# A three-sublayer block (routed attention, gated recurrence, routed attention): fp16 transposes moved from the matrix engine to the DMA queue, with a new order of the work

## The reference

```
x = x + 0.5 * ffn(layernorm(x), W_gate, W_qkv)
x = x + attn(layernorm(x), gamma, beta, W_in, b_in, W_out, b_out, W_skip, b_skip)
x = x + 0.5 * ffn(layernorm(x), W_gate, W_qkv)

ffn:   gating = softmax(x @ W_gate.T)              # 16 heads
       q, k, v = split(x @ W_qkv.T)
       k, v of the top-1 head of each row are kept (v times its gate)
       att = softmax(causal(q_h @ k_shared.T / 4)) # 16 heads of width 16
       y = att @ v_shared
attn:  u = layernorm(x) * gamma + beta
       delta, b, c = split(u @ W_in + b_in);  alpha = sigmoid(delta)
       h_t = (1 - alpha_t) h_(t-1) + alpha_t b_t;  y_t = h_t tanh(c_t)
       out = y @ W_out + b_out + x @ W_skip + b_skip
```

## Time and profile before

| | us |
|---|---|
| median of 3 runs (lowest, highest) | 844.35 (844.28, 846.64) |
| the profiled execution, its own time | 846.07 |
| its span, first to last instruction | 844.3 |
| PE matmul busy | 813.1 (96%) |
| DVE busy | 732.2 (87%) |
| ACT busy | 712.4 (84%) |
| POOL busy | 307.5 (36%) |
| mean granted TensorE clock | 0.985 of full speed |
| DMA queue of SP, share of 16 engines | 6.0% |

### The profile page before, as it was taken

One profiled execution on the slowest core, in us unless ns is written; L12 is line 12 of the kernel. 1 busy time (PEld: TensorE's weight loads), 2 busy tenths in 40 slices (PEclk: granted clock), 3 DMA queues, 4 the chain that ended last, 5 costly groups with the idle time before them and its releaser, 6 DMA issues.

```text
span 844.3 us, 18872 instructions
## 1 busy us (share of the span) xinstructions
PE 813.1 (96%) x6416; PEld 282.2 (33%) x6416; DVE 732.2 (87%) x2315; ACT 712.4 (84%) x1130; POOL 307.5 (36%) x600
## 2 busy tenths in 40 slices
PE   9999999999999999999999999999999999999997
PEld 6533333333232232324233433342223333222221
DVE  5889899899999999999738996999999899999910
ACT  1148797869999789897989898899998899999996
POOL 3235524623224433236545365631124434011010
PEclk9889799999999999999999999999999999999999
DMA  6120001111000000100020002000000100000000
GB/s 200 51 64 2 2 2 30 36 33 33 2 2 2 1 2 2 58 7 2 2 64 1 3 3 63 2 2 26 2 2 15 52 26 28 1 2 2 1 1 26
DMA packets 20254, 18.00 MB, mean 21 GB/s; under 512 B 4144, under 2 KB 20160, under 8 KB 20160
## 3 DMA queue, kind: packets, MB, share of 16 engines
q1 hardware_dynamic: 19072, 15.74, 6.0%
q10 hardware_dynamic: 1088, 1.07, 0.4%
HBM read 10.24 MB, written 6.29 MB: 20 GB/s over the span
## 4 chain that ended last, share of the span: by engine, by line
PE 57%; DVE 16%; issue 9%; ACT 9%; POOL 7%; DMA 1%; SPq 0%; POOLq 0%; ACTq 0%; DVEq 0%
PE ps L1715 19%; PE ps L1680 12%; PE ps L1703 10%; ACT probs L1191 6%; DVE mxp L1406 6%; DVE ps L1409 5%; PE ps L1598 3%; ACT relu L1175 2%; PE ps L1613 2%; POOL u L876 2%; PE ps L1646 1%; DMA q_t<-m_row 1%; POOL u_x L942 1%; DVE mxp L1409 1%; PE ps L1603 1%
## 5 line engine op out<-in xcount | busy, mean ns | idle before, releaser
L1191 ACT ACTIVATE probs<-ps 128x1024 f32<-128x1024 f32 (+4 forms) x763 | 546.6, 800 | 54.5 <-PE ps L1703 50.3
L1715 PE MATMUL ps<-probs,v_l 128*32 128x512 f32 (+3 forms) x2560 | 296.3, 544 | 1.4 <-ACT probs L1191 0.7
L1406 DVE TENSOR_REDUCE mxp<-ps 128x1 f32<-128x512 f32 x384 | 240.8, 683 | 8.9 <-PE ps L1680 5.5
L1409 DVE CUSTOM_DVE_ANT_0 ps<-ps,mask 128x384 f32<-128x384 f32 (+3 forms) x512 | 233.8, 524 | 15.5 <-PE ps L1680 14.2
L1680 PE MATMUL ps<-k_tl,q_t 48*128 48x512 f16 (+3 forms) x1152 | 227.3, 336 | 5.7 <-DVE mxp L1409 2.5
L1703 PE MATMUL ps<-q_t,k_tl 50*128 50x512 f16 (+3 forms) x1280 | 220.5, 353 | 9.6 <-DMA q_t<-m_row 2.2
L911 POOL TENSOR_SCALAR_AFFINE_SELECT probs<-probs 128x256 f32<-128x256 f32 (+1 forms) x192 | 92.4, 488 | 226.9 <-ACT probs L1191 225.0
L1409 DVE CUSTOM_DVE_ANT_0 ps<-ps,relu 128x256 f32<-128x256 f32 (+1 forms) x256 | 136.3, 587 | 5.8 <-PE ps L1680 5.0
L1680 PEld LDWEIGHTS ps<-k_tl,q_t 48*128 48x128 f16 x1152 | 70.4, 94 | 152.0 <-DVE mxp L1409 40.2
L1703 PEld LDWEIGHTS ps<-q_t,k_tl 50*128 50x128 f16 x1280 | 62.1, 94 | 176.8 <-ACT probs L1191 92.5
L1175 ACT ACTIVATE relu<-ps 128x512 f32<-128x512 f32 x192 | 108.1, 620 | 5.0 <-PE ps L1680 4.5
(11 more groups left out here) (183 smaller groups left out, 638.0 us busy)
## 6 DMA issues: line engine op xcount, KB each, us to landing
q_t<-q_scratch SPq DMA_DIRECT2D x96, 64.0 KB, 2.3
q_scratch<-q_part SPq DMA_DIRECT2D x16, 256.0 KB, 2.2
out_dram<-x_sb SPq DMA_DIRECT2D x4, 512.0 KB, 3.5
x_sb<-in_L_attn_x_dram SPq DMA_DIRECT2D x3, 512.0 KB, 5.1
q_t<-m_row SPq DMA_DIRECT2D x64, 4.0 KB
wqkv_n<-in_L_ffn_W_qkv_dram ACTq DMA_DIRECT2D x1, 768.0 KB, 5.3
w_in_sb<-in_L_attn_W_in_dram SPq DMA_DIRECT2D x1, 384.0 KB, 5.6
x_sb<-in_L_attn_x_dram ACTq DMA_DIRECT2D x1, 256.0 KB, 3.4
```

The source lines that it names most:

```text
L1191: last = a_.activation(out[:, done:done + banks], scores, ACT.Exp, scale=SCALE / LIFT ** 2)
L1406: last = v_.tensor_reduce(to, scores, axis=AX, op=ALU.max)
L1409: last = v_.tensor_tensor_reduce(scores, scores, added, 1.0, LOWEST, ALU.add, ALU.max, accum_out=to)
L1715: last = mm(out_bank[VW * hh:VW * hh + VW, P * i:QW], v_l[:, l, kt, :], probs[:, s % NB, hh, P * i:QW], start=j == 0, stop=j == key_tiles( ...
```

## The change

All fp16 transposes leave PE. A new entry `flip` transposes both halves of a normed chunk at once, by one transposing DMA issued from SP (`dma_start_transpose`, [128, 2048] fp16); `keys` and `dkeys` become transposing DMAs on SP as well (512 or 256 columns), and `row` too, for which `mx2` is widened to 128 columns; the two small DMAs that followed it are now an entry of their own, `mrow`. The copies by ACT go with them. The fp32 transposes of (0,0) and (0,1) stay on PE. POOL no longer waits for PE's transposes before it overwrites `u` or `mx2`, but for the halves or for the transposing DMA. Halves are laid out as `[2, DC, TC, 128]`, so that what the DMA reads is contiguous. The planner's durations are set anew (one line of them is shown), it has SP as an engine, and `PICKS` is a new string (2408 entries for 2389).

```
+    flipped = [("turn", l, c, 0), ("turn", l, c, 1)] if (l, c) in SINGLE \
+        else [("halve", l, c, dc) for dc in range(DC)] + [("flip", l, c)]
+    return [("stats", l, c), ("norm", l, c)] + flipped + [("gate", l, c), ("pick", l, c),
...
-    return [("stats", 2, c), ("norm", 2, c), ("halve", 2, c, 0), ("halve", 2, c, 1), ("turn", 2, c, 0), ("turn", 2, c, 1), ("bsum", c, 0), ("bsum", c, 1),
+    return [("stats", 2, c), ("norm", 2, c), ("halve", 2, c, 0), ("halve", 2, c, 1), ("flip", 2, c), ("bsum", c, 0), ("bsum", c, 1),
...
-    "gate": (1850, [("DVE", 450), ("ACT", 250)]), "pick": (0, [("DVE", 1400)]),
+    "gate": (1810, [("DVE", 395), ("ACT", 250)]), "pick": (0, [("DVE", 1550)]),
...
-TURN_MODE, ROW_TRIP, QUERY_TRIP = 97, 2300, 6000
+TURN_MODE = 97
+LANDING = {"flip": 2300, "keys": 2000, "dkeys": 2000, "row": 2000, "mrow": 2300, "qout": 2300, "qin": 2300}
...
-    "55222222222225522252555422225522205255520050240222052200552122202212201115220312420225511002112200235422222022",
+    "5zd22222225222222552252224245550252244500522002102212255522224505055042111202202102225320225104141100535022122",
...
-        rows.append(("row", u))
+        rows += [("row", u), ("mrow", u)]
...
-        mx2 = sb("mx2", [P, 2 * GH * TC], f16)
-        m_row = sb("m_row", [2 * GH * TC, 2, P], f16)
+        mx2 = sb("mx2", [P, P], f16)
+        m_row = sb("m_row", [P, 2, P], f16)
...
+                elif e[0] == "flip":
+                    _, l, c = e
+                    sp.wait_ge(s_half, NO["halve", l, c, DC - 1] + 1)
+                    if FLIP_BEFORE[e]:
+                        past = FLIP_BEFORE[e][2]
+                        sp.wait_ge(s_fill, filled(("skip", past, 1) if l == 2 else ("kv", FLIP_BEFORE[e][1], past, TC - 1)))
+                    to = u2t_x if l == 2 else ut_x
+                    sp.dma_start_transpose(to[:, :, :, :].rearrange("p a d (t x) -> p (a d t) x", x=P),
+                                           u_x[:, :, :, :, :].rearrange("p a d t x -> p (a d t x)")).then_inc(s_flip, 16)
+                elif e[0] == "keys":
+                    _, l, c = e
+                    sp.wait_ge(s_krow, prep_no(l, c) + 1)
+                    sp.dma_start_transpose(k_tl[:, l, c, :].rearrange("p (t x) -> p t x", x=P),
+                                           k_rows[:, :, :].rearrange("p t x -> p (t x)")).then_inc(s_kt, 16)
+                elif e[0] == "dkeys":
+                    _, l, c = e
+                    sp.wait_ge(s_drow, NO[e] + 1)
+                    to = (kd_tl if c else kh_tl)[:, l, :]
+                    sp.dma_start_transpose(to.rearrange("p (t x) -> p t x", x=P),
+                                           k_rows[:, 0:to.shape[1] // P, :].rearrange("p t x -> p (t x)")).then_inc(s_kt, 16)
                 elif e[0] == "row":
+                    v = e[1]
+                    sp.wait_ge(s_mx, v + 1)
+                    if v >= 2:
+                        sp.wait_ge(s_md[v % 2], 32 * (v // 2))
+                    sp.dma_start_transpose(m_row[:, v % 2:v % 2 + 1, :], mx2[:, :]).then_inc(s_row, 16)
+                elif e[0] == "mrow":
                     l, c, g = UNITS[e[1]]
-                    sp.wait_ge(s_ra, FREED[e])
+                    sp.wait_ge(s_row, 16 * (e[1] + 1))
...
-                if k:
-
-                    pool.wait_ge(s_fill, filled(TURNS[k - 1]))
+                if k and fine(*NORMS[k - 1][1:]):
+                    pool.wait_ge(s_half, NO[("halve",) + NORMS[k - 1][1:] + (DC - 1,)] + 1)
...
-                    pool.wait_ge(s_fill, filled(("row", v - 1)))
+                    pool.wait_ge(s_row, 16 * v)
...
+                if NO["flip", l, c]:
+
+                    pool.wait_ge(s_flip, 16 * NO["flip", l, c])
+                whole, first = u[:, :, dc * P:(dc + 1) * P], u_x[:, 0, dc, :, :]
                 own(g_.tensor_copy(first, whole))
-                g_.tensor_tensor(u_x[:, 1, :, dc * P:(dc + 1) * P], whole, first, op=ALU.subtract).then_inc(s_half, 1)
+                g_.tensor_tensor(u_x[:, 1, dc, :, :], whole, first, op=ALU.subtract).then_inc(s_half, 1)
...
-                elif e[0] == "turn" and fine(e[1], e[2]):
-                    dst = u2t_x if e[1] == 2 else ut_x
-                    a_.activation(dst[:, e[3], :, :].rearrange("p a t -> p (a t)"), bank[:, :].bitcast(f16), ACT.Copy)\
-                        .then_inc(s_ra, 1)
...
-                elif e[0] == "keys":
-                    _, l, c = e
-                    a_.activation(k_tl[:, l, c, :], bank[:, 0:QW // 2].bitcast(f16), ACT.Copy).then_inc(s_ra, 1)
-                elif e[0] == "dkeys":
...
-                elif e[0] == "row":
-                    v = e[1]
-                    if v >= 2:
-                        act.wait_ge(s_md[v % 2], 32 * (v // 2))
-                    a_.activation(m_row[:, v % 2, :], as_rows(bank), ACT.Copy).then_inc(s_ra, 1)
...
-                        act.wait_ge(s_fill, filled(TURNED[e]))
+                        act.wait_ge(s_kt, 16 * KEYS_FLIPPED[e])
...
                 if fine(l, c):
-                    parts = bank.bitcast(f16)
-                    for a in range(2):
-                        for t in range(TC):
-                            last = tr(parts[:, a * QW + t * P:a * QW + (t + 1) * P], u_x[:, a, t, dc * P:(dc + 1) * P],
-                                      ident_h[:, :])
-                    last.then_inc(s_fill, 1)
-                    return
...
+                    pe.wait_ge(s_flip, 16 * (NO["flip", l, c] + 1))
+                    pe.wait_ge(s_wx, 3)
...
-                if e[0] == "row":
-                    pe.wait_ge(s_mx, v + 1)
-                    tr(as_rows(bank), mx2[:, :], ident_h[:, :]).then_inc(s_fill, 1)
-                    return
                 if e[2] == 0:
                     pe.wait_ge(s_qt[prep_no(l, c)][g // 2], 16 * 2 * len(Q_PART))
-                    pe.wait_ge(s_ra, FREED["keys", l, c])
+                    pe.wait_ge(s_kt, 16 * KEYS_FLIPPED["keys", l, c])
                     if c:
-                        pe.wait_ge(s_ra, FREED["dkeys", l, min(c, 2) - 1])
+                        pe.wait_ge(s_kt, 16 * KEYS_FLIPPED["dkeys", l, min(c, 2) - 1])
```

200 lines of the change are left out of this document (92 added, 108 removed).

## The result

The changed kernel is slower: 855.3 us median (852.8 to 857.9, 4 runs) against 845.5 (844.3 to 846.8, 4 runs), a ratio of 1.0122 with a 95% interval of 1.0095 to 1.0148. That is 1.2% slower. The forecast was 826 us, faster, with a range up to 845. The profiled execution has 857.85 us (span 856.1) and was the slowest of the four.

The account below looks back on a forecast made before the run. It took PE's in-order line, held most often by exponentials, to bound the middle stretch, with DVE next. From 846.07 us, - 18.8 - 4 + 0.7 + 2 + 1.5 gave 827.5, a median of 826 us, range 808 to 845.

Parts of the forecast that it names:

- What leaves PE: Transposes leaving PE's line, mostly in the middle stretch: 18.8 us gained, taken whole, with a lower bound of 0.
- rival 3: DVE already bounds the kernel, so PE's removed work turns into waits for DVE: time stays at 844 us; chance 0.11.
- What leaves ACT: Copies of 34.2 us leave ACT, so PE waits less for exponentials: 4 us gained, between 0 and 20.
- The transposing DMA: DMA cost: 2.2 us for a row or keys, 4 us for a flip, with all ten flips hidden at no cost.
- Rival 1: Blocks of a flip go one after another on the DMA: 886 us at 1 us a block; chance 0.07.
- The first keys: At the start, the first maxima wait for keys by DMA and the warm matmuls: +0.7 us, between 0 and +2.
- The rows: Each unit's maxima reach q_t 1.3 us later by DMA, mostly with nothing waiting: +2 us before the last unit.
- The last unit's hand-off: At the kernel's end the row arrives 1.3 us later and cannot hide well: +1.5 us, between +0.8 and +3.
- Rival 2: The rows' path to qk becomes the bound, with waits for q_t above 15 us: 850 us as a case; chance 0.08.
- The new order: The new instruction order across the kernel could help or hurt: counted as 0, with 8 us either way.

Follow-up runs that it names:

- E11: Kernel before with 16 of its 20 transposed halves cut to one block of eight and nothing in their place: 844.6 us, ratio 0.998.
- E17: Kernel before with most transposed halves cut to one block of eight and exponentials shortened by an eighth from step 40 on: 838.4 us, ratio 0.990.
- E18: E6 with the rows of units 3, 4 and 28 to 31 alone transposed on PE again: 839.2 us, 0.993 of the kernel before.
- E16: Kernel before with exponentials over full blocks leaving out an eighth from step 40 on: 839.0 us, ratio 0.992.
- E1: Kernel before with its old list, but all transposes of the change done by DMA: 902.6 us, ratio 1.065.
- E2: Kernel before with its old list, only flips, keys and key differences by transposing DMA, rows still on PE: 876.4 us, ratio 1.035.
- E6: Changed kernel with four list entries moved: three statistics behind scores needing POOL's masks, unit 2's small DMAs ahead of qin: 847.2 us, 1.002 of the kernel before.
- E4: Changed kernel's new list, but with all transposes on PE and ACT as before: 893.9 us, 1.056 of the kernel before.
- E15: Kernel before with one more small DMA ahead of the transfers of a row in units 28 to 31 only: 856.6 us, ratio 1.013.
- E5: Changed kernel with 69 warm matmuls put into its eight PE gaps: 853.2 us, 1.010 of the kernel before.
- E10: E6 with maxima, join and row of units 3, 28, 30 and 31 earlier in the list: 859.0 us, 1.014 of the kernel before.

## Why the prediction was wrong

**What leaves PE: wrong, and the largest error.** The step "I take the whole, since in the middle stretch PE has 3% of idle time" read PE's busy share as work. E11 and E17 give 0.2 to 0.3 us for each microsecond removed; by estimate 18.8 us are then worth about 4 to 5, with ACT's share in it. E18, which keeps nearly all of the removal and has the new list, gains 6.2 us. The forecast had the reason in its first paragraph ("whoever is late holds the work of the others") and did not use it in the sum. Its rival 3, where removed work turns into other waits, was right on this term and had 0.11; its bound below, 0, was nearly the value. But the waits are not the ones that rival named: PE's waits for DVE grew by 3.5 us in all, those for ACT's exponentials by 19, while ACT itself waited 24 us more for PE.

**What leaves ACT: right in kind, counted too high.** 4 us were taken; in E11 the copies' part is inside the same 1.5 us. E16 shows ACT at 0.18 us for each of its own.

**The transposing DMA: right.** In the median flips landed in 4.3 and 4.7 us (4 taken; the longest took 6.1), keys in 2.5 and rows in 2.3 (2.2 taken), and the flips were hidden, with no wait for `ut_x`; E1 and E2 show that this is the new list's doing. Rival 1 is out: 16 blocks take twice as long as one. The Trainium skill's rule that such DMAs are as fast as regular ones ("Advanced Engine Details and Errata", "X-Bar Transpose (TRN2)") comes near but is not met: a flip reads 512 KB, and its 4.3 and 4.7 us are about one and a half times the 2.9 of the plain 512 KB to device memory in the same kernel. The Trainium skill's 1309 ns for one 128x128 transpose by DMA ("VectorE: DVE Perf Modes", "The three transpose paths") can't be a rate for a row of blocks, by these 4.7 us for 16. The first keys came at 32.94 us, +0.3 against +0.7.

**The rows: mis-sized, and this decides the sign.** "For most units nothing waits for those yet" is the sentence that failed. It took +2 us for 31 units. PE's waits for `q_t` alone are 8.1 us (from 2.2), their number as before; unit 2's came from SP's queue, and those of units 30 and 31 from transposing DMAs that took 4.1 to 4.4 us instead of 2.3 (see below). Putting six of the 32 rows back on PE (E18 against E6) is worth 8 us. The last unit's hand-off was 3.2 us longer instead of 1.3. Rival 2 described this place, at 850 us, and had 0.08, though its own sign, over 15 us of waits for `q_t`, did not come: few and long waits were enough.

**The new order: nothing was counted, four entries cost 8 us.** Three masks behind `stats` on POOL, and `mrow` behind `qin` on SP (E6). Against it the new list and the new mechanism together won 9 us in units 8 to 15. E4 shows that the list can't be priced alone. The prediction gave the order 8 us either way.

**Missing altogether: what follows a gap.** The sum took a wait at its own length. E15 measures the price: 7.8 us of gaps cost 12, while the clock falls behind three of the four and PE, ACT and DVE have next to no slack. In the changed kernel the eight gaps are 15.1 us and lost is 22.5 us more than before. With the idle time, 37.2 - 24.3 = 12.9 us more, that is 35.4; set against the 18.8 us of work removed, 16.6 remain, where the profiled executions are 11.8 apart. This balance counts some time twice (a slow matmul may fill a wait), so it shows the size and no more. How much of a gap's price is the clock's is not shown: E6 gained 8 us with lost nearly as it was, and E5 took 9 us off lost for a gain of 2.

What stays open: whether DVE's work paces the middle of the kernel, why E10 did not gain although the late units' gaps were gone, and how much of the loss is the clock's.
